# Attention pooling over 200 keys: key loads started by TensorE's position in its instruction stream instead of VectorE's progress

## The reference

```python
# q (2048, 128), k (2048, 200, 128), mask (2048, 200), W1 (512, 64), W2 (64, 1)
qe = jnp.broadcast_to(q[:, None, :], k.shape)
feat = jnp.concatenate([qe, k, qe - k, qe * k], axis=-1)
h = feat @ W1 + b1
h = jnp.where(h >= 0, h, alpha[0] * h)
a = (h @ W2 + b2)[..., 0]
a = jnp.where(mask == 0, jnp.float32(NEG), a)
w = jax.nn.softmax(a, axis=-1)
return jnp.einsum('bl,bld->bd', w, k)
```

## Time and profile before

| | us |
|---|---|
| three runs | 1023.59, 1003.37, 1007.28 |
| median | 1007.28 |
| the profiled execution, its own time | 1010.41 |
| its span on the core | 1008.3 |

### The profile page before, as it was taken

The page is one execution under the profiler, slowest core; times in us unless marked ns, Lnnn a source line. Parts: engine busy times, 40 slices in busy tenths (PEclk is TensorE's granted clock), DMA queues, the critical chain, the costliest instruction groups (busy, mean ns, idle before and its releaser), DMA issues.

```text
span 1008.3 us, 55360 instructions
## 1 busy us (share of the span) xinstructions
PE 852.4 (85%) x25216; PEld 560.0 (56%) x25216; DVE 769.5 (76%) x1143; ACT 533.8 (53%) x1281; POOL 656.2 (65%) x401
## 2 busy tenths in 40 slices
PE   2779889888889888889888898898898889888896
PEld 1445556555556555556555565565565556555564
DVE  5988867878878778778677778788778778777871
ACT  0556545555545555555554555565556555555552
POOL 3667656767667667667666676676676666667761
PEclk9999999999999999999899999999999999999999
DMA  8847667667677767677665777666777666777620
GB/s 256 338 145 229 217 231 234 230 221 246 198 240 244 231 218 238 201 237 242 232 202 180 239 235 236 213 216 231 239 242 242 231 213 209 242 262 235 225 94 11
DMA packets 67017, 222.45 MB, mean 221 GB/s; under 512 B 25312, under 2 KB 33504, under 8 KB 66784
## 3 DMA queue, kind: packets, MB, share of 16 engines
q1 hardware_dynamic: 66784, 218.92, 65.5%
HBM read 214.57 MB, written 4.33 MB: 217 GB/s over the span
## 4 chain that ended last, share of the span: by engine, by line
PE 38%; DMA 18%; DVE 16%; issue 13%; ACT 7%; SPq 7%; POOL 0%; DVEq 0%; ACTq 0%; POOLq 0%
PE hP L435 22%; DMA keys<-in_r_k 11%; DVE act L350 9%; PE poolP L478 8%; PE scoreP L466 7%; DMA probs_scratch<-expd 6%; ACT act L289 5%; DVE keysT L342 5%; SPq L160 3%; SPq L211 3%; ACT expd L315 2%; DVE neg_max L363 1%; PE poolP L487 1%; DVE logits L357 1%; DMA keys<-in_r_q 1%
## 5 line engine op out<-in xcount | busy, mean ns | idle before, releaser
L289 ACT ACTIVATE act<-hP,biast,al 128x200 f32<-128x200 f32 x1024 | 460.3, 514 | 352.7 <-PE hP L435 349.1
L342 DVE STREAM_TRANSPOSE keysT<-keys 128x768 f32<-128x768 f32 (+1 forms) x512 | 510.0, 997 | 60.8 <-DMA keys<-in_r_k 60.6
L435 PE MATMUL hP<-keysT,weff 32*64 32x200 f32 x16384 | 482.8, 346 | 38.3 <-issue 30.3
L232 POOL TENSOR_TENSOR weff<-qX,wp 128x1024 f32<-128x1024 f32 x128 | 243.9, 1906 | 315.6 <-PE hP L435 299.7
L435 PEld LDWEIGHTS hP<-keysT,weff 32*64 32x64 f32 x16384 | 312.7, 134 | 201.5 <-issue 129.3
L350 DVE TENSOR_TENSOR act<-hP,act 128x400 f32<-128x400 f32 x512 | 283.8, 554 | 144.8 <-ACT act L289 140.7
L236 POOL TENSOR_TENSOR weff<-weff,wk 128x1024 f32<-128x1024 f32 x128 | 303.3, 2369 | 10.0
L478 PE MATMUL poolP<-keys,pool_w 128*16 128x128 f32 x6400 | 242.7, 276 | 18.4 <-issue 16.9
L478 PEld LDWEIGHTS poolP<-keys,pool_w 128*16 128x16 f32 x6400 | 172.7, 97 | 91.4 <-issue 86.7
L466 PE MATMUL scoreP<-act,w2win 128*16 128x200 f32 x2048 | 150.0, 342 | 73.9 <-DVE act L350 69.8
L271 POOL TENSOR_TENSOR pool_w<-probs_k,own_b 128x400 f32<-128x400 f32 x128 | 111.2, 869 | 15.7 <-PE poolP L478 7.9
(11 more groups left out here) (35 smaller groups left out, 29.7 us busy)
## 6 DMA issues: line engine op xcount, KB each, us to landing
keys<-in_r_k SPq DMA_DIRECT2D x128, 832.0 KB, 5.7
keys<-in_r_k SPq DMA_DIRECT2D x128, 768.0 KB, 5.2
probs_scratch<-expd SPq DMA_DIRECT2D x32, 100.0 KB, 4.0
masks<-in_r_mask SPq DMA_DIRECT2D x128, 12.5 KB
probs_k<-probs_scratch SPq DMA_DIRECT2D x128, 12.5 KB
out_rows<-pooled SPq DMA_DIRECT2D x128, 8.0 KB
keys<-in_r_q SPq DMA_DIRECT2D x4, 256.0 KB, 5.1
act<-in_L_rec_W SPq DMA_DIRECT2D x4, 128.0 KB, 6.4
```

What stands on the lines that cost most here:

```text
L232: g_.tensor_tensor(weff[:, n % 2, :, :, :], qX[:, n, :, :].unsqueeze(3).broadcast_to([P, BQ, CD, H]), wp[:].unsqueeze(1).broadcast_to([P, ...
L289: a_.activation(act[:, k, a, :], hP[:, 2 * (p % HSETS) + a % 2, 0:L], ACT.Identity, bias=biast[:, n, k, a:a + 1], scale=al[:]).then_inc(t_ ...
L342: v_.transpose(keysT[:, n % TBUF, j0 * D:j1 * D], keys[:, n % SLOTS, j0 * D:j1 * D]).then_inc(keysT_done, 1)
L435: mm = t_.matmul(hP[H * r:H * r + H, 2 * (p % HSETS) + a % 2, 0:L], weff[QP * a:QP * a + QP, n % 2, w, c, :], kT[QP * a:QP * a + QP, :, c, ...
```

## The change

It concerns when key loads are started, in what sizes, and what VectorE waits for.

- TensorE's program is moved ahead of SP's in the file (each engine still has its own program) and counts the instructions that it sends: four for a `matmul` call and one for every two waits ahead of it, from 65 (BLOCK_AT) at the start. Each time the count passes a multiple of 256 (BLOCK) the next of certain matmuls increments the semaphore `block_begun`, and the place in steps, in units of 392 instructions (STEP_LEN), is put into the list `begun`. That gives 190 entries for steps 4 to 127, 0.653 of a step apart in the mean.
- SP's steady loop runs over this list instead of over steps. At each entry it waits for `block_begun` and then issues two parts of the keys, or three where it is behind (`many`), or none where the slot is not yet free by the count (`free_at`).
- The keys come in three parts, rows 0 to 8, 9 to 17, 18 to 24 (576, 576 and 448 KB). For three tiles of four the first part may start when the first 12 pooling matmuls of the tile in the slot are done (`head_done`), about half a step sooner than before.
- The write of the exponentials goes ahead of the keys of the first entry at or behind step 4(g + 1) + 0.5; the wait for its landing and the reads follow the keys of that entry. Masks follow the keys of the first entry at or behind 4(g + 1) + 2.0, outputs at or behind 4(g + 1) + 6.7.
- VectorE waits at each piece only for the part that the piece newly touches: piece 0 for part 0, piece 1 for part 1, piece 3 for part 2.

Matmuls, transposes and all arithmetic stay what they are, in the same order on their engines.

```diff
-LOADS = 2
-LOAD_CUT = [0, 12, J]
+LOAD_CUT = [0, 9, 18, J]
+LOADS = len(LOAD_CUT) - 1
+LANES = 4
+BLOCK = 256
+BLOCK_AT = 65
+STEP_LEN = 392
...
+            waits, sent, blocks, step = 0, BLOCK_AT, 0, (0, 0)
...
+                    pe.wait_ge(sem, value)
+                    waits += 1
...
+                sent += waits // 2 + 4
+                waits = 0
+                return t_.matmul(*args, **flags)
...
+                new = sent // BLOCK > blocks
+                blocks = sent // BLOCK
+                if new and GT <= step[0] < TILES:
+                    begun.append(step[0] + (sent - step[1]) / STEP_LEN)
+                    return True
+                return False
...
+                        if r == 0 and a % 2 == 0 and in_new_block():
+                            mm.then_inc(block_begun, 1)
...
+                mm.then_inc(part_done if j1 == J else head_done, 1)
...
-                        behind = PIECES * (n + 1) + 2 + x * PIECES // LOADS
-                        sp.wait_ge(keysT_done, min(behind, PIECES * TILES))
-                        load_part(n + AHEAD, x)
...
+            write_at = [first_at(GT * (g + 1) + 0.5) for g in range(GROUPS)]
+            mask_at = [first_at(GT * (g + 1) + 2.0) for g in range(GROUPS)]
+            out_at = [first_at(GT * (g + 1) + LAG + 0.7) for g in range(GROUPS)]
+            last = len(begun)
+
+            part = SLOTS * LOADS
+            for b, at in enumerate(begun):
+
+                sp.wait_ge(block_begun, b + 1)
+                for g in range(GROUPS):
+                    if write_at[g] == b:
+                        write_probs(g)
+                for y in range(LOADS):
+                    n, x = part // LOADS, part % LOADS
+                    m = n - SLOTS
+                    many = (math.floor(at) + AHEAD + 1) * LOADS - part > LOADS
+                    early = x == 0 and m % GT > 0
+                    free_at = m + LAG + 0.45 if early else m + LAG + 0.96
+                    if n >= TILES or at < free_at or (y == LOADS - 1 and not many):
+                        break
+                    if early:
+
+                        sp.wait_ge(head_done, m + 1 - m // GT)
+                    else:
+                        sp.wait_ge(part_done, m + 1)
+                    load_part(n, x)
+                    part += 1
+                for g in range(GROUPS):
+                    if write_at[g] == b:
+                        read_probs(g)
+                    if mask_at[g] == b and g + 2 < GROUPS:
+                        sp.wait_ge(scores_read, g + 1)
+                        load_mask(g + 2)
+                    if out_at[g] == b:
+                        write_out(g)
...
+                for x in range(LOADS):
+                    if CUTS[piece] <= LOAD_CUT[x] < CUTS[piece + 1]:
+                        dve.wait_ge(keys_in[n % LANES][x], (n // LANES + 1) * 16)
                 if piece == 0:
-                    dve.wait_ge(keys_in[n % SLOTS], (n // SLOTS + 1) * 16 * LOADS)
                     ge(dve, main_done, PAIRS * (n + 1 - TBUF))
```

More of the change, by code:

```diff
@@ L1 @@
+import math
 from contextlib import ExitStack
@@ L104, in attention_pooling @@
         poolP = ps("poolP", [P, 512])
-        keys_in = [sem(f"keys_in{x}") for x in range(SLOTS)]
+        keys_in = [[sem(f"keys_in{y}_{x}") for x in range(LOADS)] for y in range(LANES)]
+        block_begun = sem("block_begun")
+        head_done = sem("head_done")
         mask_in = [sem(f"mask_in{x}") for x in range(2)]
@@ L151, in load_part @@
                 at = slice(LOAD_CUT[x] * D, LOAD_CUT[x + 1] * D)
-                sp.dma_start(keys[:, n % SLOTS, at], k_tiles[n][:, at]).then_inc(keys_in[n % SLOTS], 16)
+                sp.dma_start(keys[:, n % SLOTS, at], k_tiles[n][:, at]).then_inc(keys_in[n % LANES][x], 16)
             def load_keys(n):
@@ L176, in _ @@
                 if n > 2:
-                    sp.wait_ge(keys_in[n - 2], 16 * LOADS)
+                    for x in range(LOADS):
+                        sp.wait_ge(keys_in[(n - 2) % LANES][x], ((n - 2) // LANES + 1) * 16)
                 if n == 3:
@@ L184, in _ @@
                 load_keys(n)
-            for n in range(STEPS):
-                def paced_part(x):
-                    if SLOTS <= n + AHEAD < TILES:
-                        behind = PIECES * (n + 1) + 2 + x * PIECES // LOADS
-                        sp.wait_ge(keysT_done, min(behind, PIECES * TILES))
-                        load_part(n + AHEAD, x)
[L194 to L221, removed]
@@ new lines, in first_at, with write_probs, read_probs @@
+            def first_at(place):
+                return sum(at < place for at in begun)
+            def write_probs(g):
+                sp.wait_ge(exp_done, g + 1)
+                ge(sp, poolw_done, (g - 1) * GT)
+                sp.dma_start(probs_dram[g % 2], expd[:, g % 2, :]).then_inc(probs_out, 16)
+            def read_probs(g):
+                sp.wait_ge(probs_out, (g + 1) * 16)
+                for t in range(GT):
+                    sp.dma_start(probs_k[:, g % 2, t, :], probs_tiles[g % 2, t]
+                                 ).then_inc(probs_in[GT * (g % 2) + t], 16)
@@ new lines, in write_out @@
+            def write_out(g):
+                sp.wait_ge(pooled_moved, g + 1)
+                for c in range(QUADS):
+                    sp.dma_start(out_rows[g, c], pooled[QP * c:QP * c + HALF_Q, g % 2, :]
+                                 ).then_inc(out_done[g % 2], 16)
+            write_at = [first_at(GT * (g + 1) + 0.5) for g in range(GROUPS)]
+            mask_at = [first_at(GT * (g + 1) + 2.0) for g in range(GROUPS)]
+            out_at = [first_at(GT * (g + 1) + LAG + 0.7) for g in range(GROUPS)]
@@ L222, in _ @@
+            assert part == TILES * LOADS
+            for g in range(GROUPS):
+                if write_at[g] == last:
+                    write_probs(g)
+                    read_probs(g)
+            for g in range(GROUPS):
+                if out_at[g] == last:
+                    write_out(g)
             for x in range(2):
@@ L423, in _ @@
                 activate(PAIRS * n + 2)
[L425 to L518, removed]
-                if n == TILES:
-                    first_layer(PAIRS * n)
-                if late and m <= TILES:
-                    add_parts(m // GT - 1)
-                if 0 <= m < TILES and not late:
-                    pool_keys(m, 0, HEAD_J)
-                if 0 <= n - 1 < TILES:
-                    second_layer(n - 1, 1)
-                if n < TILES:
-                    first_layer(PAIRS * n + 2)
-                    first_layer(PAIRS * n + 3)
-                if 0 <= m < TILES:
-                    pool_keys(m, 0 if late else HEAD_J, J)
-                if n < TILES:
-                    second_layer(n, 0)
```

110 lines of the change are left out of this document (added).

## The result

| | before | after |
|---|---|---|
| median us | 1008.40 (4 runs, 1003.37 to 1023.59) | 949.38 (4 runs, 944.73 to 955.37) |
| ratio | | 0.945, 95% interval 0.939 to 0.951 |
| span of the profiled execution | 1008.3 | 944.5 |
| mean granted TensorE clock | 0.979 | 0.992 |

The forecast was 958 with a range of 925 to 1000. Six runs more, in a later set with its own runs of the kernel before, gave 945.64 against 1011.80 (0.935, interval 0.928 to 0.941). Medians are over all runs, while ratios leave out those over 1.5% above the fastest of the same kernel.

A forecast was written before the change was run, and what follows sets the result against it. No engine was full; TensorE, nearest at 85%, lost 49.2 us waiting for issue and VectorE 60.6 us for keys. Gains of (10 + 52) x 0.79 = 49 us from 1007.3 gave 958 us, range 925 to 1000.

The forecast's parts named there:

- Block, border and counter: TensorE's instructions come in blocks of 256, the next fetched when one begins; the count hits borders, signal under 0.4 us behind.
- write and reads: SP's queue, once a group: exponentials' write and four reads delay the next keys, pausing TensorE; mean 1.0 us, 31 us in all.
- The pauses that remain: TensorE's matmul waits for issue: 39 us left of 49.2, 31 behind the writes and 8 elsewhere; 10 us gained.
- none elsewhere: Sign on TensorE: nearly all remaining issue waits, near 39 us, stand one or two blocks behind the exponentials' write.
- Waits of VectorE: VectorE's waits for key loads fall from 60.6 to some 8 us: 52 gained, bounds 30 to 60.6.
- GpSimd's wait for probabilities: GpSimd gets the probabilities about in time; cost taken as 0, bound 0.5 us in 6 groups.
- The split of the sum: Gain on TensorE's issue pauses, 10 us, plus VectorE's key waits, 52 us, times 0.79: 49 us.
- factor of 0.79: Share of each us of TensorE's issue idle and VectorE's key waits that is in the time: 87 / 109.8.
- The ceiling: Most that better timed key loads can give, from undisturbed step periods: 87 us, so 920 us.
- Traded: Rival: keys start on time but TensorE pauses at every block as two parts outlast it; 1027 or 996 us; 0.19 with nothing.
- Both go: Rival: late keys behind the reads delay no fetch, pauses fall to 8 us; 931 us, 920 at best; chance 0.18.
- Slower by lead: Rival: key parts paced by TensorE's signal land too late for VectorE, 149 us of waits; 1077 us; chance 0.07.

The follow-up runs named there:

- experiment 4: Changed kernel with the signal shifted 128 instructions, to mid-block: 1020.37 us, ratio 1.015; or to 64 instructions ahead of the border: 1015.99 to 1040.66 us, no ratio.
- Experiment 1: Kernel before, with only VectorE's wait changed, from the whole tile to the part (of two) that a piece newly touches: 1014.83 us, ratio 1.000.
- write later (6): Changed kernel with the write of the exponentials from 0.75 instead of 0.5 of the step: 942.06 us, ratio 0.931; repeated 949.89 us, ratio 0.939.
- experiment 6: Changed kernel with the exponentials' write on ScalarE's queue, SP's landing wait and reads from 0.9 or 0.6 of the step: 959.06 or 955.32 us, both ratio 0.947.
- experiment 2: Kernel before with keys in three parts, all ahead of the write: 1021.37 us, ratio 1.013; second kernel, also with VectorE waiting by part: 1024.04 us, ratio 1.013.
- experiment 3: Changed kernel with VectorE again waiting for all three parts of a tile ahead of its first piece: 954.73 us, ratio 0.946.

## Why the prediction was right, and where it was not

**Block, border and counter: right.** Instructions come in blocks of 256, and the count from 65 hits the border: a shift of half a block costs all of the gain (experiment 4). That a fetch is asked for at the border fits every run, though no trace shows the asking. In the changed kernel a remaining pause shows the same mechanism as the earlier trace rows. PE's weight loads (127 of them from the first line to the pause), then SP's queue, then the DMA queues in 651.7 to 655.2 and in 655.2 to 656.5:

```profile
651.69 0.56 PEld L174 LDWEIGHTS poolP<-keys,pool_w 128*16 128x16 f32 x21 [0.57 <-issue]
...
657.83 0.91 PEld L174 LDWEIGHTS hP<-keysT,weff 32*64 32x64 f32 x46 [1.41 <-issue]
```

```profile
646.29 2.42 SPq L351 DMA_DIRECT2D probs_k<-probs_scratch  x4
648.80 4.15 SPq L303 DMA_DIRECT2D keys<-in_r_k  x4
```

```profile
q1 hardware_dynamic: 280, 1.09, 95.7%
```

```profile
q1 hardware_dynamic: 143, 0.47, 94.0%
q8 instruction: 1, 0.02, 4.6%
```

The reads of the probabilities hold SP until 648.7. The two parts of keys that belonged to the block before follow at 648.80 and about 651.1, just ahead of the border at 651.69: the first one's issue took 2.17 us of SP's queue, where the prediction had 0.33 for each (the median of all 384 is 0.43, the longest 3.09). Then 1.09 MB of keys pass with no instruction packet, it comes over 3.5 us into the block, and PE's weight loads stand idle 1.41 us until 657.83. This is the step "write and reads" of the prediction, as it was described, with SP's slow issue on top.

**The pauses that remain: 29.6 us measured, 39 predicted, and placed wrong.** The prediction had 31 us behind the writes, in all 31 groups, and 8 us elsewhere. By the timeline of the matmuls 17 pauses, 14.8 us together, stand 5 to 16 us behind a write, in 12 of the groups; the other 22, another 14.8 us, stand elsewhere, 3.6 us of them at the start and the end of the span. The share of the write is half of what was forecast: the write lands in 2.6 us, not the 3.67 taken from the earlier trace rows, so the hold is a us shorter, and most groups pay nothing. The sign asked for was "none elsewhere", and that failed.

**Waits of VectorE: 0 measured, 8 predicted.** The leads of 1.78 steps and more were enough; a part lands in 5.1 us at the median.

**GpSimd's wait for probabilities: taken as 0.** It rose from 7.8 us, once at the start, to 22.8 in 10 times, over the bound of 3 us. TensorE's matmuls wait 1.2 us for `pool_w` before and 1.4 after, so it cost little or nothing.

**The split of the sum: wrong, and this is the step that failed.** The prediction gave 41 us (52 x 0.79) to VectorE's waits and 8 (10 x 0.79) to fetches. Experiment 1 removes 57 of the 60.6 us of waits without a gain in the median, and experiment 4 has no such waits and no gain. The factor of 0.79 treated the two idle times as alike and independent. They stand in one another's shadow: take VectorE's away alone, and pauses grow to 80 us. Against that kernel the gain is the fall from 80 to 29.6, and the signal's place brings it. The total came nearly right, partly because the ceiling of 87 us bounded it, and partly by luck: as the reckoning below has it, one term was too high and two were too low or left out.

**The ceiling: right.** 920 was worked out from the earlier trace rows; without key loads the kernel takes 916.39.

**What does add up** is shown by the runs in which VectorE hardly waits for keys. Take from the span the issue idle and the lost clock, (1 - granted clock) x span:

| run | span | issue idle | lost clock | rest |
|---|---|---|---|---|
| no key loads (5) | 914.1 | 4.0 | 0.006 x 914.1 = 5.5 | 904.6 |
| changed kernel | 944.5 | 29.6 | 0.008 x 944.5 = 7.6 | 907.3 |
| before, wait by part (1) | 998.6 | 79.6 | 0.016 x 998.6 = 16.0 | 903.0 |
| before, three parts, wait by part (2) | 1015.9 | 78.3 | 0.033 x 1015.9 = 33.5 | 904.1 |
| signal mid-block (4) | 1018.6 | 87.8 | 0.010 x 1018.6 = 10.2 | 920.6 |
| signal ahead of the border (4) | 1038.9 | 117.4 | 0.015 x 1038.9 = 15.6 | 905.9 |
| changed kernel, second profile | 942.4 | 26.9 | 0.005 x 942.4 = 4.7 | 910.8 |
| write later (6), first profile | 944.6 | 28.8 | 0.010 x 944.6 = 9.4 | 906.4 |
| write later (6), second profile | 948.5 | 27.6 | 0.008 x 948.5 = 7.6 | 913.3 |

Eight of nine lie within 903 to 913.3, and the same kernel profiled twice differs by 3.5 and 6.9 us, so the reckoning is good to some 7 us; mid-block keeps some 13 us more than the changed kernel, which it doesn't account for. The two kernels of experiment 6 with the write on ScalarE's queue leave 925.3 and 914.8. From 4.0 to 117.4 us of issue idle the rest stays the same (904.6 and 905.9): by this, each us of these pauses is a us of time, not 0.79. By this reading experiment 2's second kernel is 17 us longer than experiment 1's with the same idle time because its clock was lower (0.967 against 0.984).

For the kernel before the same reckoning leaves 1008.3 - 49.2 - 21.2 - 906 = 32, give or take the 7, so about half of VectorE's 60.6 us stood on the path. The first kernel of experiment 2 gives the same (31 of 65.4), and experiment 3 about 10 of 29.4. So from before to after about 32 us come from VectorE's waits (predicted 41), 49.2 - 29.6 = 19.6 from pauses (predicted 8), and 21.2 - 7.6 = 14 from the clock, which was no term of the prediction; together 65, and the span fell by 63.8. It is a reckoning and not a recipe: in experiment 1 the first of these, taken alone, came back as pauses.

**The rivals.** "Traded" did not happen in the changed kernel, but it is what experiments 1 and 4 show: waits gone, pauses up, time as before. "Both go" rested on smaller parts letting fetches through; experiment 2 is against it. The Trainium skill ("DMA: Bandwidth & Descriptors", Arbitration) has an engine serve its queues in turn, a packet from each; the 78.3 us with parts of 576 KB against 79.6 with 832 KB show no such effect of the size of a load. How an engine's queues take turns was not measured: the traces show when a packet was moved and not when it was asked for, and in the window of the earlier trace rows that lacks TensorE's fetch a packet of another instruction queue did pass (q14, 1 packet, 0.01 MB). "Slower by lead" found nothing: no wait for keys at all.

## What to carry to other kernels

Where a long unrolled program keeps TensorE busy, count its instructions between idle times for "issue". If they are multiples of 256, as here, suspect that the instruction fetch waits for data, and try starting large loads just behind a block's border and not ahead of it. Two idle times on different engines with one cause (here the same DMA queues) must not be priced as a sum: remove one alone and see whether the other grows. A part of a change that is worth nothing by itself may still belong to it, so try the full change with one thing undone before crediting any part.

## What the runs showed of the hardware beyond expectation

- With key loads in flight the packet with the next instruction block came more than 3.5 us into the block before it, and TensorE resumed 1.1 us or more after the packet; without them issue idle was 4.0 us in a whole run with as many blocks.
- Moving the same loads by half a block of 4.5 us, with their order, sizes and bytes unchanged, cost 7% (949.38 and 1020.37 us, ratios 0.945 and 1.015).
- The granted clock of otherwise like kernels ran from 0.967 to 0.995 in the profiled executions. It wasn't the idle time in total that cost clock: the two lowest are the three-part kernels paced by VectorE (0.967 both) with issue idle of 48.6 and 78.3 us, while mid-block, with 87.8 us in 108 pauses of at most 2.1 us, had 0.990. The traces show what did. In experiment 2's second kernel TensorE stood idle 2.20 us until 379.00 and 3.30 until 865.89; behind each of these the granted clock was 0.50 (1.2 GHz) for a stretch, then full again (2.4 GHz). These rows are windows, with the busy time and instructions of PE, PEld, DVE, ACT and POOL, then PEclk, the DMA share and GB/s:

```profile
379.60:382.80 3.20, 3.20 (x76) 2.15 (x80) 0.73 (x2) 1.25 (x3) 1.58 (x1) 0.50 0.93 365
383.50:387.50 4.00, 3.71 (x114) 2.46 (x114) 3.35 (x6) 2.13 (x5) 2.90 (x2) 1.00 0.42 125
...
868.00:870.50 2.50, 2.50 (x68) 1.97 (x64) 0.97 (x2) 0.78 (x2) 0.00 (x0) 0.50 0.59 238
```

  The changed kernel's longest pause, 2.77 us until 246.24, was followed by the same (0.50 in 246.6 to 249.6). So a long single pause is paid twice, and the changed kernel has fewer of them than that one. Not each is: the longest of its second profile, 2.21 us, was not.
